# First-layer statistics and the block maxima of one matrix moved among the first products, and a wait ahead of the first weight split

## The chip, the cores and the metric

The kernel runs on one core of a Trainium2 chip. The metric is the device time of one execution in microseconds (us). The kernel before takes 1513.26 us, the median of 3 runs (1510.02 to 1513.64).

## The reference, cut to what matters

The program is a stack of four layers, each an attention and a feed-forward block with a layer norm ahead and a residual add behind, over x of 4 x 256 tokens x 512 features. The change touches two things: the first layer norm and attention (layer 0), and the dequantisation of the last feed-forward's weights (layer 3), which the kernel computes in the background of layer 0.

```python
def _layernorm(x, axis=-1, eps=1e-05):
    m = jnp.mean(x, axis=axis, keepdims=True)
    v = jnp.var(x, axis=axis, keepdims=True)
    return (x - m) / jnp.sqrt(v + eps)

def nf4_quant_dequant(w):                      # BLOCKSIZE = 64
    shape = w.shape
    flat = w.reshape(-1, BLOCKSIZE)
    absmax = jnp.max(jnp.abs(flat), axis=1, keepdims=True)
    normalized = flat / jnp.where(absmax == 0, 1.0, absmax)
    bounds = (NF4_CODE[:-1] + NF4_CODE[1:]) * 0.5
    idx = jnp.searchsorted(bounds, normalized)
    return (NF4_CODE[idx] * absmax).reshape(shape)

x = x + _L0_xattn_ref(_layernorm(x), ctx_4096, L0_xattn_Wq, L0_xattn_Wk, L0_xattn_Wv, L0_xattn_Wo)
...
dq1, dq2, dq3 = nf4_quant_dequant(w1), nf4_quant_dequant(w2), nf4_quant_dequant(w3)   # 1376 x 512 each
```

Layer 0's attention has 16 query heads in 4 groups of width 96, and each batch element has 256 + 64 keys.

## The kernel before

**Order of the work.** `schedule()` writes one list of steps by hand. Each engine walks that list and issues, in this order, what it has to do for a step. All engines are strictly in order on their own list and meet through semaphores. Tokens are in 8 tiles of 128, in two halves of 4 tiles. The list begins with `("stats", 0, 0)`, `("turn", 0, 0)`, six `v0` steps (value projections of four token tiles and two context parts), `k0`, `kc0` (keys of group 0), `q0` for 4 heads (numbered 0 to 3), and then the attention units n = 0, 1, 2, ...: `scores0` (scores on TensorE, maxima on VectorE, exp on ScalarE), `scale0` (VectorE), `turn0` (transposes on TensorE), `pv0`. After unit 2's scores the keys `k0` of the next group are computed. A `stats` step is VectorE work: `bn_stats` of 4 tiles, `bn_aggr`, a chain of about a dozen operations on 128 x 4 elements for 1/sqrt (the function `rsqrt`, lines 1199 to 1205), and the four normalisations into `xn` (line 1238). `turn` is transposes of `xn` on TensorE (line 1751), with a high part by ScalarE and a low part by VectorE (line 1194) into `xT`.

**Products.** Every fp32 product is done in three passes of rounded high and low parts (line 1724). So every weight chunk is loaded by SyncE into one of two staging buffers (line 743), its high part is made by ScalarE (line 951, `weight_high`), and its low part by GpSimd (line 858, `weight_low`). This pair is called a split. There are five slots for split chunks. SyncE issues the load of chunk i when chunk i-2 has its low part. Chunks 0 and 1 are the weights of `v0`, chunk 2 is the context, 3 and 4 are the weights of `k0`, `kc0` and `q0` of group 0, 5 and 6 those of group 1, 7 and 8 the output weights. `v0`'s first product waits for the low parts of both chunk 0 and chunk 1. The place of each split in the list is set by `spread_splits`: for the early ones, chunk i (i = 2 to 5) stands behind the list's entry number i-1, counted from zero, whatever that entry is.

**Background.** The dequantisation is a list `jobs`. For matrix m: `nf_row` (SyncE loads 128 rows, 256 KB, into one of four buffers; for the fifth row and on it waits until the maxima of four rows before are done, line 757), `nf_max` (VectorE, maxima of the 8 blocks of each row, line 1636; behind the last one a reciprocal, line 1641), `nf_turn` (TensorE transposes the maxima, line 2082, and waits for that reciprocal; ScalarE copies; SyncE stores them to HBM), `nf_scales` and `nf_load` (SyncE loads them back, broadcast, with the transposed weights, lines 792, 805, 807), then 15 `nf` steps for each of 33 tiles (VectorE, line 1664; ahead of the very first one 15 factor tiles `nf_d`, line 1647), each with an `nf_sum` product (TensorE, line 2093).

`with_background(base, "q0", BACKGROUND_END, jobs)` merges them into the list, starting behind the first `q0` step. Each step of the list has a room, each job a price (`NF_PRICE`: 1 for `nf`, 1.2 for `nf_max`, 6 for matrix 0's last one, 11 for the first `nf_load`, 0 for rows, `nf_turn` and `nf_scales`), and jobs are put in as long as what is paid is below the bill (the sum of prices) times the share of the room that is spent. The rooms sum to 511.64 and the bill to 550.4. That puts the eleven maxima of matrix 0 between the `q0` steps and ahead of the first scores, `nf_turn` for matrix 0 behind the next group's `k0`, and the first `nf` step behind the transposes of unit 3. `("stats", 0, 1)`, the statistics of x's second half, stands in the list ahead of `scores0` of unit 4.

Of the kernel before, what the change touches and what calls it, by code (L numbers as in the profile page):

```python
# [19 lines left out]
TPH = TILES // 2  # L20
BPH = B // 2
# [86 lines left out]
def schedule(only=None):  # L108

    steps = []  # L110


    steps += [("stats", 0, 0), ("turn", 0, 0)]
    steps += [("v0", 0, i) for i in range(TPH + BPH)]
    steps += [("k0", 0), ("kc0", 0)] + [("q0", 0, h) for h in range(HPG)]
    units = [(s, bl, h) for s in range(2 * G0) for h in range(HPG) for bl in range(BPH)]
    per, last_stage = HPG * BPH, 2 * G0 - 1
    for n in range(len(units) + PV_LAG):
        if n < len(units):
            steps.append(("scores0", n, *units[n]))  # L120
        if 1 <= n <= len(units):
            steps.append(("scale0", n - 1))
        if TURN_LAG <= n < len(units) + TURN_LAG:
            steps.append(("turn0", n - TURN_LAG, *units[n - TURN_LAG]))
        if n >= PV_LAG:
            steps.append(("pv0", n - PV_LAG, *units[n - PV_LAG]))
            if n - PV_LAG == G0 * per - 1:
                steps += [("v0", 1, i) for i in range(TPH + BPH)]
        if n < len(units):
            s, j = n // per, n % per  # L130
            if s < last_stage:
                late = 4 if s == G0 else 2
                if j == late:
                    steps.append(("k0", s + 1))
                if j == late + 1:
                    steps.append(("kc0", s + 1))
            if s >= 1 and j in (3, 4):
                steps += [("o0", s - 1, i) for i in (2 * j - 6, 2 * j - 5)]
            if s < last_stage and j >= 5:
                steps += [("q0", s + 1, h) for h in ((0, 1), (2,), (3,))[j - 5]]  # L140
            if (s, j) == (0, 3):
                steps.append(("stats", 0, 1))
            if (s, j) == (1, 2):
                steps.append(("turn", 0, 1))
            if (s, j) == (G0, 6):
                steps.append(("stats", 1, 0))
            if (s, j) == (G0 + 1, 6):
                steps.append(("turn", 1, 0))
# [204 lines left out]
def build(nc, a, out, known, only=None):  # L353
    ctx = ExitStack()
    with ctx:
        sig = Signals(nc, ctx, known)
# [36 lines left out]
        k0 = sb("k0", [HD0, 2, 2, BPH, KEYS0], F32R, s0)  # L393
# [186 lines left out]
        base = schedule(only)  # L580
        normalisations = [s[1:] for s in base if s[0] == "stats"]
        if only is None or only == 7:
            jobs = []
            jobs += [("nf_row", 0, f) for f in range(4)]
            for f in range(FT):
                jobs += [("nf_max", 0, f)] + [("nf_row", 0, f + 4)] * (f + 4 < FT)
            jobs.append(("nf_turn", 0))
            rest, rows = [], [("nf_row", m, f) for m in range(1, 3) for f in range(FT)]
            for m in range(1, 3):
                rest += [[("nf_max", m, f)] for f in range(FT)] + [[("nf_turn", m)]]  # L590
            rest[0] = rows[0:3] + rest[0]
            for entry in rest:
                if entry[-1][0] == "nf_max" and entry[-1][1:] != (1, 0):
                    i = (entry[-1][1] - 1) * FT + entry[-1][2]
                    entry[:0] = rows[i + 2:i + 3]
            items = [(m * FT + f, m, f) for m in range(3) for f in range(FT)]
            jobs += [("nf_scales", *items[0]), ("nf_load", *items[0])]
            sums = []
            for n, m, f in items:
                for j in range(1, NPART + 1):  # L600
                    jobs.append(("nf", n, m, f, j))
                    sums.append(("nf_sum", n, m, f, j))
                    if j > STAIR_RING - 1 or not n:
                        while len(sums) > STAIR_LAG:
                            jobs.append(sums.pop(0))
                    if j == 2 and n:
                        jobs += sums[:-2] + [("nf_end", *items[n - 1])]
                        sums = sums[-2:]
                    if j == 4 and n:
                        jobs.append(("nf_store", *items[n - 1]))  # L610
                    if j == 1 and n + 1 < len(items):
                        jobs.append(("nf_scales", *items[n + 1]))
                    if j == 6 and n + 1 < len(items):
                        jobs.append(("nf_load", *items[n + 1]))
                    if n >= REST_FROM and j % 5 == 4 and rest:
                        jobs += rest.pop(0)
            jobs += sums + [("nf_end", *items[-1]), ("nf_store", *items[-1])]
            base = with_background(base, "q0", BACKGROUND_END, jobs)
            assert base.index(("turn", 0, 1)) < base.index(("nf_row", 1, 0))
            assert base.index(("nf_turn", 2)) < base.index(("stats", 1, 0))  # L620
# [220 lines left out]
        def _(pool):  # L841
# [10 lines left out]
                    pool.dma_start(dst, src).then_inc(*sig.mark(f"loaded_{name}", 0, 16))  # L852

            def split(i):
                pool.wait_ge(*sig.when("weight_high", i))
                _, p, dims, *_ = chunks[i]
                hi, lo = weight(chunks[i][0], 0), weight(chunks[i][0], 1)
# [1321 lines left out]
```

## Time and profile before

| | |
|---|---|
| median of 3 runs | 1513.26 us |
| the profiled execution | 1513.1 us, span 1511.4 us |
| TensorE busy | 1366.7 us (90%) |
| VectorE busy | 1002.1 us (66%) |
| ScalarE, GpSimd busy | 474.3 us (31%), 328.1 us (22%) |
| mean granted TensorE clock | 0.949 |
| chain that ended last | PE 67%, DVE 18%, DMA 4% |

The span is the stretch from the first to the last instruction; the execution's own time is 1.7 us longer. In the rows PE is TensorE, DVE VectorE, ACT ScalarE, POOL GpSimd, SP SyncE. PEclk 1.00 is a granted clock of 2.4 GHz and 0.50 one of 1.2 GHz. The change lies wholly in the first 95 us of the list, so its own stage has to be read and not the averages.

### The profile page before, as it was taken

How to read it: one execution, taken by the hardware profiler on the slowest of the kernel's cores; microseconds unless marked ns; L12 is line 12 of the kernel's file. 1: busy time of each engine (PE TensorE's matmuls, PEld its weight loads, DVE VectorE, ACT ScalarE, POOL GpSimd, SP SyncE). 2: the span in 40 equal slices, each digit the busy share in tenths (PEclk: the TensorE clock that was granted, in tenths of full speed). 3: DMA queues.
4: the chain of work that ended last, by engine and by line, in shares of the span. 5: the costliest groups of instructions: out<-in, count | busy, mean ns of one | idle time of the engine just before them, and what ended most of it. 6: DMA issues, size and time to landing. Idle time of an engine off the chain costs nothing.

```text
span 1511.4 us, 18615 instructions
## 1 busy us (share of the span) xinstructions
PE 1366.7 (90%) x6429; PEld 1055.8 (70%) x6429; DVE 1002.1 (66%) x2200; ACT 474.3 (31%) x1004; POOL 328.1 (22%) x187
## 2 busy tenths in 40 slices
PE   6689999999999989997797889778999899999998
PEld 5467676777676766886675676556887677778886
DVE  3577878767878667876988667675446777444242
ACT  3333334333324233341344141322221443321010
POOL 4101211112111111342224140214443230012120
PEclk9889999999999999999899799879999999899999
DMA  4412433323322222332322220100112000011001
GB/s 153 144 39 77 112 116 111 107 77 95 90 80 78 68 77 83 86 113 86 109 81 82 85 84 1 56 29 16 43 54 70 28 29 2 1 49 63 25 20 56
DMA packets 112559, 104.86 MB, mean 69 GB/s; under 512 B 14674, under 2 KB 84194, under 8 KB 112466
## 3 DMA queue, kind: packets, MB, share of 16 engines
q1 hardware_dynamic: 111954, 102.81, 23.2%
q8 instruction: 54, 0.88, 0.2%
q0 software_dynamic: 512, 0.85, 0.2%
q14 instruction: 39, 0.32, 0.1%
HBM read 92.79 MB, written 10.82 MB: 69 GB/s over the span
## 4 chain that ended last, share of the span: by engine, by line
PE 67%; DVE 18%; DMA 4%; issue 3%; ACT 3%; SPq 3%; POOL 2%; ACTq 0%; DVEq 0%
PE bank L1724 49%; PE bank L2093 5%; PE bank L1818 4%; DVE nf_y L1664 4%; PE bank L2028 2%; PE bank L2048 2%; PE bank L1808 2%; POOL slots L858 2%; DVE xn L1238 1%; SPq L807 1%; PE bank L1751 1%; SPq L792 1%; ACT slots L951 1%; PE bank L2037 1%; DVE nf_w L1658 1%
## 5 line engine op out<-in xcount | busy, mean ns | idle before, releaser
L858 POOL TENSOR_TENSOR slots<-staging,slots 128x1024 fp32r<-128x1024 f32 (+5 forms) x114 | 269.0, 2364 | 1025.7 <-ACT slots L951 1025.7
L1724 PE MATMUL bank<-xT,slots 128*128 128x512 f32 (+1 forms) x1920 | 462.0, 398 | 4.5 <-DVE xT L1247 3.2
L1724 PEld LDWEIGHTS bank<-xT,slots 128*128 128x128 f32 (+1 forms) x1920 | 349.0, 183 | 103.5 <-issue 10.8
L1664 DVE TENSOR_SCALAR nf_y<-nf_w 128x512 fp32r<-128x512 f32 (+2 forms) x495 | 254.1, 550 | 21.1 <-PE bank L2093 20.0
L951 ACT ACTIVATE slots<-staging 128x1024 fp32r<-128x1024 f32 (+5 forms) x114 | 115.2, 1018 | 251.1 <-PE bank L1724 217.5
L2093 PE MATMUL bank<-nf_y,nf_d 128*128 128x512 f32 (+2 forms) x495 | 160.9, 418 | 36.2 <-DVE nf_y L1664 20.5
L1724 PE MATMUL bank<-slots,h 128*128 128x512 f32 (+1 forms) x728 | 178.9, 406 | 0.7 <-POOL slots L858 0.7
L1724 PEld LDWEIGHTS bank<-slots,h 128*128 128x128 f32 (+1 forms) x728 | 141.3, 195 | 36.3 <-issue 1.8
L2093 PEld LDWEIGHTS bank<-nf_y,nf_d 128*128 128x128 f32 (+1 forms) x495 | 92.1, 192 | 75.0 <-DVE nf_y L1664 39.1
L985 ACT ACTIVATE e<-bank,mx 128x320 f32<-128x320 f32 x128 | 66.4, 523 | 227.4 <-DVE mx L1275 225.3
L1294 DVE TENSOR_TENSOR x<-bank,x 128x512 f32<-128x512 f32 x56 | 38.7, 692 | 112.7 <-PE bank L1724 112.7
L1818 PE MATMUL bank<-eT,v 128*96 128x256 f32 (+1 forms) x384 | 109.3, 406 | 0.1
L1724 PE MATMUL bank<-slots,q 96*128 96x512 f32 x384 | 95.2, 397 | 0.0
L1194 DVE TENSOR_TENSOR q<-bank,q 96x256 fp32r<-96x256 f32 (+1 forms) x96 | 48.6, 506 | 57.8 <-ACT q L938 57.8
L1724 PEld LDWEIGHTS bank<-slots,q 96*128 96x128 f32 x384 | 71.8, 188 | 18.4 <-issue 1.5
L1818 PEld LDWEIGHTS bank<-eT,v 128*96 128x96 f32 (+1 forms) x384 | 57.0, 169 | 33.9 <-issue 24.7
L1751 PE MATMUL bank<-ident,xn 128*128 128x128 f32 x256 | 45.4, 323 | 34.7 <-DVE xn L1238 31.3
L1808 PE MATMUL bank<-ident,e 128*128 128x128 f32 x256 | 49.0, 287 | 28.0 <-DVE e L1282 25.8
L1724 PE MATMUL bank<-k,q 96*128 96x320 f32 x384 | 69.1, 316 | 3.3 <-DVE q L1194 3.1
L1724 PEld LDWEIGHTS bank<-k,q 96*128 96x128 f32 x384 | 61.8, 192 | 9.2 <-DVE q L1194 3.6
L1751 PEld LDWEIGHTS bank<-ident,xn 128*128 128x128 f32 x256 | 35.3, 163 | 45.3 <-issue 34.3
L938 ACT ACTIVATE q<-bank 96x256 fp32r<-96x256 f32 (+1 forms) x96 | 42.8, 449 | 62.4 <-PE bank L1724 58.6
(250 smaller groups left out, 1673.4 us busy)
## 6 DMA issues: line engine op xcount, KB each, us to landing
staging<-in_L_wqkT SPq DMA_DIRECT2D x16, 480.0 KB, 3.6
nf_out<-nf_w SPq DMA_DIRECT2D x30, 256.0 KB, 2.7
staging<-nf_out SPq DMA_DIRECT2D x30, 256.0 KB, 2.9
staging<-in_L_woT SPq DMA_DIRECT2D x16, 384.0 KB, 3.7
staging<-in_L_w SPq DMA_DIRECT2D x12, 512.0 KB, 3.7
nf_r<-nf_rcp SPq DMA_DIRECT2D x40, 128.0 KB, 3.1
nf_a<-nf_max SPq DMA_DIRECT2D x40, 128.0 KB, 3.5
xn<-in_L_w SPq DMA_DIRECT2D x20, 256.0 KB, 3.7
```

What stands on the lines that cost most here:

```text
L858: g.tensor_tensor(lo, split_source(i), hi.bitcast(FP32), ALU.subtract).then_inc(*sig.mark("weight_low", i))
L938: sc.activation(dst, src, func, **kw).then_inc(*sig.mark(f"{stage}_high", key))
L951: sc.activation(weight(name, 0), split_source(i), ACT.Copy).then_inc(*sig.mark("weight_high", i))
L985: sc.activation(e0[:, (2 * n + i) % E0_RING], psum(("scores0", n, i))[:, 0:KEYS0], ACT.Exp, bias=mx[:, n % 4, i:1 + i], accum_out=sm[:, n ...
L1194: v.tensor_tensor(dst, src, hi.bitcast(FP32), ALU.subtract).then_inc(*sig.mark(f"{stage}_low", key))
L1294: v.tensor_tensor(x[:, t], src, x[:, t], ALU.add).then_inc(*sig.mark(*mark))
L1664: v.tensor_scalar(nf_y[0:rows, i % STAIR_RING, 0:size], w_, bound, first, compare, ALU.mult)\
L1724: ins = mm(dst, l_, r_, start=begin and i == 0, stop=end and i == len(passes) - 1)
L1751: ins = nc.tensor.transpose(bank[:, i * P:(i + 1) * P], xn[:, i, c * P:(c + 1) * P], ident[:])
L1808: nc.tensor.transpose(b0[:, (2 * k + i) * P:(2 * k + i + 1) * P], e0[:, (2 * n + i) % E0_RING, k * P:(k + 1) * P], ident[:])
L1818: ins = mm(bank[0:HD0, 0:S], v0[0:p, t, g * HD0:(g + 1) * HD0], eT0[0:p, n % 2, k], start=k == 0, stop=k == 2)
L2093: mm(banks[NF_BANK][0:rows, 0:size], nf_d[0:rows, j - 1, 0:rows], nf_y[0:rows, i % STAIR_RING, 0:size], start=j == 1, stop=j == NPART).the ...
```

## The change

Three edits. `("stats", 0, 1)` moves from ahead of unit 4's scores to behind the third `v0` step. The 22 jobs `nf_row` and `nf_max` of matrix 0 are taken off the front of the background list and put by hand behind the first steps: four rows behind the first `v0` step; behind the fourth, fifth and sixth `v0` steps two maxima and two rows each; behind `k0` the maxima 6 and 7 with row 10 between them; behind `kc0` the maxima 8, 9 and 10. The rest of the list, beginning with `nf_turn`, is merged from the first `q0` step on as before, with a bill that is smaller by their prices. GpSimd's first split waits until the last tile of the first half is normalised.

```diff
-    steps += [("v0", 0, i) for i in range(TPH + BPH)]
+    steps += [("v0", 0, i) for i in range(3)] + [("stats", 0, 1)] + [("v0", 0, i) for i in range(3, TPH + BPH)]
...
-            if (s, j) == (0, 3):
-                steps.append(("stats", 0, 1))
...
             for f in range(FT):
                 jobs += [("nf_max", 0, f)] + [("nf_row", 0, f + 4)] * (f + 4 < FT)
+
+            places = {("v0", 0, 0): 4, ("v0", 0, 3): 4, ("v0", 0, 4): 4, ("v0", 0, 5): 4, ("k0", 0): 3, ("kc0", 0): 3}
+            base = [entry for s in base for entry in [s] + [jobs.pop(0) for _ in range(min(places.get(s, 0), len(jobs)))]]
+            assert not jobs
             jobs.append(("nf_turn", 0))
...
             def split(i):
+                if i == 0:
+                    pool.wait_ge(*sig.when("normalised", (0, TPH - 1)))
                 pool.wait_ge(*sig.when("weight_high", i))
```

## Rows read from the trace of the kernel before

**Rows 1.** Busy time by stretch: us, PE, PEld, DVE, ACT, POOL, PEclk, DMA share, GB/s.
```profile
45.80:60.20 14.40, 3.77 (x19) 2.89 (x18) 12.23 (x24) 3.42 (x9) 2.36 (x1) 0.63 0.62 199
60.20:63.30 3.10, 3.08 (x11) 2.45 (x12) 1.72 (x6) 2.36 (x9) 0.00 (x0) 0.51 0.00 0
...
73.80:79.30 5.50, 0.02 (x1) 0.05 (x1) 5.03 (x19) 1.24 (x5) 0.00 (x0) 0.78 0.34 94
79.30:87.10 7.80, 7.80 (x21) 4.84 (x22) 5.69 (x25) 3.15 (x10) 0.00 (x0) 0.50 0.06 19
```

**Rows 2.** Timeline, 45 to 80 us: start, length, engine, line, work, idle before it.
```profile
47.62 2.36 POOL L858 TENSOR_TENSOR slots<-staging,slots 96x1024 fp32r<-96x1024 f32 x1 [5.94 <-ACT slots L951]
...
48.58 0.67 DVE L1636 TENSOR_REDUCE nf_m<-nf_a 128x8 f32<-128x512 f32 x1
...
51.52 1.17 PE L1724 MATMUL bank<-k,q 96*128 96x320 f32 x3 [2.04 <-DVE q L1194]
...
57.24 0.70 DVE L1641 RECIPROCAL nf_m<-nf_m 128x88 f32<-128x88 f32 x1
57.86 1.61 DVE L1275 TENSOR_REDUCE mx<-bank 128x1 f32<-128x320 f32 x4
...
60.22 0.66 PE L1808 MATMUL bank<-ident,e 128*128 128x128 f32 x2 [7.52 <-DVE e L1282]
...
65.11 0.38 PE L2082 MATMUL bank<-ident,nf_m 128*88 128x128 f32 x2
...
70.21 2.46 DVE L1217 BATCH_NORM_STATS2 st<-x 128x6 f32<-128x512 f32 x4
...
72.62 1.23 SPq L807 DMA_DIRECT2D nf_a<-nf_max  x2
```

**Rows 3.** Timeline, 9 to 18 us, the end of the first statistics.
```profile
9.33 3.56 POOL L858 TENSOR_TENSOR slots<-staging,slots 128x768 fp32r<-128x768 f32 x2 [7.79 <-ACT slots L951]
9.34 1.82 DVE L1203 TENSOR_TENSOR rt<-rs 128x4 f32<-128x4 f32 x1
...
11.19 1.72 DVE L1204 TENSOR_TENSOR rt<-rt 128x4 f32<-128x4 f32 x1
...
13.15 1.91 DVE L1238 TENSOR_SCALAR xn<-x,mv,rs 128x512 f32<-128x512 f32 x4
...
17.80 9.06 PE L1724 MATMUL bank<-slots,xT 128*128 128x384 f32 x48
```

**Rows 4.** Timeline, 22 to 46 us, the first splits and products.
```profile
26.82 4.49 POOL L858 TENSOR_TENSOR slots<-staging,slots 128x960 fp32r<-128x960 f32 x2 [2.38 <-ACT slots L951]
...
30.86 2.95 PE L1724 MATMUL bank<-xT,slots 128*96 128x512 f32 x12
...
34.64 11.32 PE L1724 MATMUL bank<-xT,slots 128*96 128x512 f32 x48
```

**Rows 5.** DMA issues in 0 to 100 us: count, KB, median us to landing.
```profile
staging<-in_L_wqkT SPq DMA_DIRECT2D x6, 480.0 KB, 4.1
nf_w<-in_L_w SPq DMA_DIRECT2D x6, 256.0 KB, 3.8
...
x<-in_x SPq DMA_DIRECT2D x1, 1024.0 KB, 7.1
...
nf_a<-nf_max SPq DMA_DIRECT2D x4, 128.0 KB, 3.6
```

**Rows 6.** Timeline at 880 us: normalisations beside a split.
```profile
880.78 3.97 DVE L1238 TENSOR_SCALAR xn<-x,mv,rs 128x512 f32<-128x512 f32 x4
...
880.95 2.61 POOL L858 TENSOR_TENSOR slots<-staging,slots 128x1024 fp32r<-128x1024 f32 x1 [0.23 <-ACT slots L951]
```

**Rows 7.** Timeline, 82 to 91 us, the first background steps.
```profile
82.14 2.12 DVE L1647 TENSOR_SCALAR nf_d<-ident 128x128 fp32r<-128x128 f32 x15
...
84.18 0.69 DVE L1658 TENSOR_TENSOR nf_w<-nf_w,nf_r 128x512 f32<-128x512 f32 x1
...
89.48 1.08 DVE L1664 TENSOR_SCALAR nf_y<-nf_w 128x512 fp32r<-128x512 f32 x3
```

**Rows 8.** Waits of TensorE, 110 to 620 us: total, times, longest.
```profile
PE bank L1808 <- DVE e L1282: 12.8, 12, 1.9
```

## The prediction

> **What bounds the kernel now.** I first looked at the busy time by engine: TensorE is busy for 90% of the span and most of the chain that ended last, so what counts is the time that TensorE loses, by idling or by running at the lower granted clock. Then I cut the first 95 us into stretches [rows 1]. From 45.8 to 60.2 us TensorE is busy for 3.8 of 14.4 us, and VectorE for 12.2. The timeline shows why [rows 2]: the eleven block maxima, fed by row loads, stand on VectorE ahead of the maxima of the first scores, and the reciprocal behind them ends at 57.9 us. Only then come four score maxima, and TensorE's first transposes start at 60.2. From 73.8 to 79.3 TensorE idles again: the statistics of the second half, begun at 70.2 us, stand ahead of a score maximum [rows 1, 2]. Behind each hole the granted clock is at its lower level, 1.2 GHz (0.50): until 63.3 us, and from 79.3 to 87.1 [rows 1]. A third loss is at the start: the first product begins at 17.8 us, and just before, two VectorE operations on 128 x 4 elements took 1.82 and 1.72 us beside GpSimd's two splits [rows 3], where their like takes 0.16 to 0.17.
>
> I count in lost TensorE time, against the profiled execution of 1513.1 us. It lies 0.2 us below the median of the runs, so no correction is needed.
>
> **What the change takes away.**
> - Start. Without the splits beside them the two slow operations take 0.17 each, so the normalisations end 3.2 us earlier, at 15.06 - 3.2 = 11.9. The two splits, 3.56 us together [rows 3], now begin there and end at 15.5. The first product needs both, and starts at 15.6 in place of 17.8 (its other input, the transposed x, is ready from about 13.8): 2.2 us gained.
> - The hole from 45.8 to 60.2: 14.4 - 3.8 = 10.6 us idle, and 0.6 us, half of the 1.17 that three products of unit 2 took there at the lower clock [rows 1, 2].
> - The lower clock behind it, half of 3.1: 1.5. The hole of the statistics: 5.5. The lower clock behind that one, half of 7.8: 3.9 [rows 1].
>
> Together 2.2 + 10.6 + 0.6 + 1.5 + 5.5 + 3.9 = 24.3 us.
>
> **What it adds: the transposes of the maxima.** Pricing the maxima at nothing has a consequence that decides the sum. They are no longer in the background list, so that list begins with `nf_turn`, of price 0, and it is placed directly behind the first `q0` step. TensorE is in order: `q0` for heads 1 to 3 and all scores are queued behind a wait for the reciprocal of the eleven maxima. So I must find when that is ready.
>
> - Loads on SyncE. The low part of chunk 1 is done at 15.5, then chunk 3 and the 1 MB rest of x are issued; the latter lands 7.1 us later [rows 5], at 23.0. The context's split ends at about 21, chunk 3's at 23.2, chunk 4's (issued at 21, 3.6 us to land, 1 us on ScalarE, 2.25 us on GpSimd, half of 4.49 [rows 4]) at 27.9, and chunk 5's at 30.2. Row 0 is issued behind the load of chunk 5, at 23.7, row 1 behind that of chunk 6 at 28.3, rows 2 and 3 behind that of chunk 7, which waits for chunk 5's low part, at 30.6 and 31.1. At 3.8 us each [rows 5] rows 2 and 3 land at 34.5 and 35.
> - Statistics on VectorE. They begin at 23.0, `bn_stats` takes 2.46 [rows 2] and the aggregation 0.4, to 25.9. Then the small operations meet the splits of chunks 4, 5 and 6 (25.65 to 27.9, 28 to 30.2, 32.6 to 34.85). If each split holds VectorE as in [rows 3], the small ones end at 32.4. The normalisations are held too: four took 3.97 us beside a split at 880 us [rows 6] in place of 1.91 [rows 3]. They end at 36.0. If nothing held them all would end at 30.1.
> - Maxima. They are not held: one took 0.67 us inside a split at 47.6 [rows 2]. From 36.0 the first four end at 38.7. Row 6 is issued when maxima 2 are done, 38.1; it lands at 42, maxima 6 end at 43.3; row 10 follows chunk 9's load at 43.8, lands at 47.6, its maxima end at 48.3 and the reciprocal at 49.2. With statistics that end at 30.1 the landing of row 2 at 34.5 sets it, and the reciprocal ends at 45.8; with each of the three landings in this chain 1 us slower, at 52.
>
> The first `q0` step ends at about 35.3: before, `k0`, `kc0` and it took from 30.86 to 37.5 [rows 4], now they start at 28.6 (`v0` needs 13.1 us as before, and chunk 4 is ready at 27.9). So TensorE idles for 49.2 - 35.3 = 13.9 us, with 10.5 and 16.7 as ends. The load that the maxima hide behind is hidden, but TensorE is stopped for them in another place.
>
> The GPSIMD Engine Reference of the Trainium skill (section 8, Key points) says that GpSimd shares its SBUF interfaces with VectorE, with contention for instructions in a 2-port mode or with two SBUF inputs. It speaks against this change, since it would hold the moved statistics; the trace agrees for two-input operations (1.82 us) and for normalisations (3.97 us for four). By that rule the reciprocal comes at 49.2, without it at 45.8.
>
> **What it adds: the first background steps.** The bill falls by 10 x 1.2 + 6 = 18, to 532.4, or 1.041 per unit of room. The three remaining `q0` steps have 3.12 of room each, so at the fourth, 12.48 x 1.041 = 13.0 exceeds `nf_load`'s 11 and two `nf` steps stand ahead of the first score maxima; before, they stood behind unit 3. VectorE meets their weights there. From `nf_turn` (65.1) to the landing of the last broadcast (issued up to 73.85, and 3.6 to land) were about 11.7 us [rows 2, 5], so they are there at 61. TensorE ends the three `q0` steps (2.83 each [rows 4]) at 49.2 + 0.4 + 8.5 + 2.7 for the lower clock = 60.8. Copy and low part of the last follow to 62.1, and then 2.12 us for the factor tiles, to 64.2 [rows 7]: the landing is hidden. To the first transposes: 0.69 for the scaling, five `nf` steps of 0.36 that stand before and between the maxima [rows 7], and 2.36 us from the first score maximum to the transposes as before (57.86 to 60.22 [rows 2]), 4.9 in all, to 69.1. TensorE has scores and two sums until 64.0: idle for 5.1 us. The clock: a restart cost 1.5 us once and 3.9 the other time [rows 1]; I take 2.7 behind each of the two holes.
>
> Added: 13.9 + 2.7 + 5.1 + 2.7 = 24.4. The sum is 24.4 - 24.3 = +0.1, and the time 1513.2 us. The `nf` steps and sums that now run between 65 and 95 us are no cost: they are missing later. Over the rest of the background each step of the list carries 3.3% fewer of them. TensorE waits 12.8 us there for `scale0`, which `nf` steps delay [rows 8]; a thirtieth of that is 0.4. Which `nf` step meets which split changes throughout; the longest such wait was 1.9 us, and I allow 2.5 either way.
>
> **Rivals.**
> - Faster, 0.27: the statistics mostly miss the splits and the clock returns as after 60.2. Then 10.5 + 1.5 + 5.1 + 1.5 = 18.6 against 24.3, 5.7 less, 1507.4. For it: `nf_max` and `bn_stats` are insensitive, and the places depend on when x lands. Against it: three splits lie within 9 us, just where the small operations are.
> - Slower, 0.27: `nf_turn` is the new barrier and comes late. SyncE queues rows among four chunk loads, which wait for splits, and landings of 4.1 and 7.1 us show that big loads slow each other [rows 5]. With the reciprocal at 52 and 3.9 us for each restart: 16.7 + 3.9 + 5.1 + 3.9 = 29.6, 5.3 more, 1518.4. Every us by which the reciprocal comes later costs one; at the clock costs of my sum it is slower by over 0.3% from 53.6 us on, at the larger ones from 51.2.
> - The wait doesn't do what it says, 0.06: if the small operations were slow for another reason, the splits would start at 15.1 and the first product at 18.7, 3.1 us later than in my sum: 1516.3.
>
> **How the numbers follow.** My forecast, 0.40: 1513.2, with 1509 to 1517 as its own range. The range over the cases runs from 1504.9 (the faster case less 2.5) to 1519.8 (the slower one and 1.4). What this measurement can tell from no change is about 0.3%, 4.5 us. Faster: the 0.27, and 0.06 from the edge of the forecast, 0.33. Slower: 0.22 of the slower case, and 0.04 from the others, 0.26. The rest, 0.41, is no change.
>
> **What would show it.** In the trace after: the first product near 15.6 us; the statistics of the second half end between 30 and 36, with long small operations; TensorE idle from about 35 until line 2082 near 49; a second hole of about 5 us ahead of the first transposes near 69, with the factor tiles between; no hole for statistics behind unit 2. I am wrong if `nf_turn` isn't what stops TensorE, if the reciprocal is ready before 44 or after 54, or if the time differs while the first 100 us do not.

## The result, and the profile after

The kernel after takes 1502.88 us, the median of 9 runs (1499.56 to 1508.47), against 1511.31 us (1507.69 to 1514.86) for the kernel before on the same chip: a ratio of 0.9946 [0.9929, 0.9962]. That is 0.54% faster, 8 us, where I forecast no change and a range that ended at 1504.9. The profiled execution after took 1502.41 us, so the traces differ by 10.7 us; in what follows they are compared with each other, and every such difference carries the scatter of two single executions. How large that can be is shown under the last experiment: two executions with the same list up to a point reached it 9.2 us apart. From the page after (busy us, share of the span, instructions; then shares of the chain that ended last):

```profile
span 1500.7 us, 18616 instructions
PE 1359.8 (91%) x6429; PEld 1049.6 (70%) x6429; DVE 1004.3 (67%) x2200; ACT 473.5 (32%) x1004; POOL 331.5 (22%) x187
PE 65%; DVE 20%; ACT 4%; DMA 4%; issue 3%; SPq 2%; POOL 2%; ACTq 0%; DVEq 0%
```

In the code after, line numbers from 858 on are 4 higher than before (L1724 is L1728, L1664 is L1668, L2082 is L2086), and those of SyncE's loads 2 higher (L807 is L809). The start, from the timeline after (start, us, engine, line, operation, what ended the idle time before it); it answers to [rows 2, 3]:

```profile
9.84 0.16 DVE L1207 TENSOR_TENSOR rt<-rs 128x4 f32<-128x4 f32 x1
12.43 3.59 POOL L862 TENSOR_TENSOR slots<-staging,slots 128x768 fp32r<-128x768 f32 x2 [10.89 <-DVE xn L1242]
16.12 8.58 PE L1728 MATMUL bank<-slots,xT 128*128 128x384 f32 x48 [0.86 <-POOL slots L862]
26.86 2.24 POOL L862 TENSOR_TENSOR slots<-staging,slots 128x960 fp32r<-128x960 f32 x1 [2.96 <-ACT slots L955]
26.92 2.20 DVE L1207 TENSOR_TENSOR rt<-rs 128x4 f32<-128x4 f32 x1
30.53 2.17 DVE L1209 SCALAR_TENSOR_TENSOR rs<-rt,rs 128x4 f32<-128x4 f32 x1
32.74 1.92 DVE L1242 TENSOR_SCALAR xn<-x,mv,rs 128x512 f32<-128x512 f32 x4
48.23 0.70 DVE L1645 RECIPROCAL nf_m<-nf_m 128x88 f32<-128x88 f32 x1
48.98 0.66 PE L2086 MATMUL bank<-ident,nf_m 128*88 128x128 f32 x2 [12.93 <-DVE nf_m L1645]
61.01 4.53 POOL L862 TENSOR_TENSOR slots<-staging,slots 96x1024 fp32r<-96x1024 f32 x1 [21.00 <-ACT slots L955]
63.37 2.79 DVE L1668 TENSOR_SCALAR nf_y<-nf_w 128x512 fp32r<-128x512 f32 x2
69.39 0.66 PE L1812 MATMUL bank<-ident,e 128*128 128x128 f32 x2 [2.94 <-DVE e L1286]
```

The barrier of the forecast is there: TensorE idles 12.93 us ahead of line 2086 (13.9 forecast), and the moved statistics meet the splits (2.20 and 2.17 us for operations that take 0.16 alone). The stretches around both new holes (us, then busy us and instructions of PE, PEld, DVE, ACT, POOL, granted clock, share of the DMA engines, GB/s), which answer to [rows 1]:

```profile
35.50:49.00 13.50, 0.57 (x4) 0.12 (x2) 8.40 (x15) 1.70 (x3) 4.09 (x2) 0.62 0.72 231
49.00:53.40 4.40, 4.40 (x14) 3.08 (x15) 0.47 (x1) 0.44 (x2) 0.00 (x0) 0.60 0.09 20
62.00:69.40 7.40, 0.59 (x2) 0.23 (x2) 7.33 (x19) 2.25 (x8) 3.53 (x1) 0.78 0.34 101
69.40:73.00 3.60, 3.60 (x12) 2.78 (x13) 2.03 (x7) 2.62 (x7) 0.00 (x0) 0.50 0.01 1
73.00:100.00 27.00, 27.00 (x143) 20.10 (x142) 18.18 (x51) 11.19 (x33) 2.26 (x1) 1.00 0.27 74
```

The second hole is 6.8 us of 7.4, and the granted clock is back at 1.00 from 73.0. So the start went nearly as forecast, and the gain isn't there. I read the same event in both traces (for a unit, its first score maximum) and took the difference; minus is earlier than the kernel before:

```
event (time before, us)    after  e4_old  e5_merge  e1_old  e2_old  e3_no  e7_price  e9_price  e6_turn
                                  _merge  _alone    _stats  _maxima _wait  12        20        _late
unit 8 (110.7)             +3.1   -4.9    +18.0     +12.8   -9.8    +4.0   +5.9      +1.3      -12.4
unit 32 (314.1)            -4.9   -4.3    +9.9      +4.7    -8.3    -4.1   -4.1      +5.2      -14.9
first up0 step (617.4)     -1.7   -2.7    +13.4     +5.2    -5.4    -0.9   -4.1      +7.1      -15.7
867.0                      -10.2  -3.9    +5.2      -3.0    -7.9    -9.4   -13.5     +1.7      -23.6
end (1511.4)               -10.7  -4.2    +4.4      -3.7    -9.3    -10.0  -14.3     +1.3      -27.6
```

At unit 8 the kernel after is 3.1 us behind, and at 867, some 10 us behind the last of the background's sums, 10.2 ahead. All of the gain, 13.3 us, lies in between, where I had priced the change at 0.4. The same stretch in both kernels (columns as above), before and then after:

```profile
110.70:867.00 756.30, 694.97 (x3230) 527.20 (x3229) 578.80 (x1247) 268.82 (x628) 151.01 (x70) 0.96 0.32 91
```

```profile
113.90:856.80 742.90, 687.94 (x3215) 521.76 (x3214) 570.85 (x1229) 267.97 (x628) 152.11 (x70) 0.97 0.32 91
```

TensorE idles for 61.3 us before and 55.0 after, 6.4 less, and is busy for 7.0 less. It has 17 sums fewer to do here (476 before, 459 after, by line 2093 and its like), done ahead of unit 8; I price them at 4.1 (17 at 0.24, line 1728's busy time over its number on the page, an estimate). The remaining 3 go with the clock, 0.97 for 0.96.

### The profile page after: what moved, and what is told of

Same layout as the page of the kernel before. It is cut to its first block, busy times and chain, and to the rows that moved or that the text cites. A ratio compares the mean times of both kernels' runs of the same rounds, so it can differ in the third digit from the quotient of the medians.

```text
span 1500.7 us, 18616 instructions
## 1 busy us (share of the span) xinstructions
PE 1359.8 (91%) x6429; PEld 1049.6 (70%) x6429; DVE 1004.3 (67%) x2200; ACT 473.5 (32%) x1004; POOL 331.5 (22%) x187
## 4 chain that ended last, share of the span: by engine, by line
PE 65%; DVE 20%; ACT 4%; DMA 4%; issue 3%; SPq 2%; POOL 2%; ACTq 0%; DVEq 0%
PE bank L1728 47%; PE bank L2097 6%; DVE nf_y L1668 5%; PE bank L1822 4%; PE bank L2032 2%; POOL slots L862 2%; PE bank L2052 2%; PE bank L1812 1%; DVE xn L1242 1%; SPq L809 1%; ACT slots L955 1%; PE bank L2041 1%; DVE st L1315 1%; DVE x L1300 1%; DMA nf_a<-in_L_w 1%
## 5 line engine op out<-in xcount | busy, mean ns | idle before, releaser
L1728 PE MATMUL bank<-xT,slots 128*128 128x512 f32 (+1 forms) x1920 | 462.3, 398 | 6.1 <-DVE xT L1251 3.3
L1728 PEld LDWEIGHTS bank<-xT,slots 128*128 128x128 f32 (+1 forms) x1920 | 349.1, 183 | 103.8 <-issue 11.5
L1668 DVE TENSOR_SCALAR nf_y<-nf_w 128x512 fp32r<-128x512 f32 (+2 forms) x495 | 257.6, 553 | 16.6 <-PE bank L2097 15.4
L1728 PE MATMUL bank<-slots,h 128*128 128x512 f32 (+1 forms) x728 | 179.6, 407 | 0.0
L1728 PEld LDWEIGHTS bank<-slots,h 128*128 128x128 f32 (+1 forms) x728 | 142.0, 196 | 35.2 <-issue 0.4
L1822 PE MATMUL bank<-eT,v 128*96 128x256 f32 (+1 forms) x384 | 105.5, 395 | 1.1 <-ACT eT L999 1.1
L1728 PE MATMUL bank<-slots,q 96*128 96x512 f32 x384 | 95.0, 396 | 0.6 <-DVE q L1198 0.6
L1728 PEld LDWEIGHTS bank<-slots,q 96*128 96x128 f32 x384 | 71.8, 188 | 18.5 <-issue 1.7
L1728 PE MATMUL bank<-k,q 96*128 96x320 f32 x384 | 66.8, 310 | 0.0
L1728 PEld LDWEIGHTS bank<-k,q 96*128 96x128 f32 x384 | 61.0, 188 | 4.7 <-issue 0.7
L1621 DVE TENSOR_TENSOR g<-bank,g 128x512 f32<-128x512 f32 (+1 forms) x22 | 15.2, 691 | 67.2 <-PE bank L1728 67.2
```

What stands on the lines that cost most here:

```text
L1668: v.tensor_scalar(nf_y[0:rows, i % STAIR_RING, 0:size], w_, bound, first, compare, ALU.mult)\
L1728: ins = mm(dst, l_, r_, start=begin and i == 0, stop=end and i == len(passes) - 1)
L1822: ins = mm(bank[0:HD0, 0:S], v0[0:p, t, g * HD0:(g + 1) * HD0], eT0[0:p, n % 2, k], start=k == 0, stop=k == 2)
```

## The experiments

**Placement undone, placement alone.** Which part moves the middle: the edited start, or the new places of the background steps that follow from it?

```
after, NF_PRICE:   ("nf_load", 0, 0): 11   ->  29        (e4_old_merge: nf steps where they stood before)
before, NF_PRICE:  ("nf_max", 0, 10): 6    ->  **{("nf_max", 0, f): 0 for f in range(11)}
                                                         (e5_merge_alone: nf steps where they stand after)
```

> The changed kernel with the price of the first nf_load raised from 11 to 29, which is the 18 that the moved maxima took out of the bill. From the first nf step on, the background is then merged with the foreground exactly as in the kernel before (same bill, same places), while the early statistics, the early maxima, nf_turn behind the first q0 and the wait of the first split stay. Theory START (the gain comes from the lost TensorE time of the first 100 us, as my accounting had it): the hole of 13.9 us and one restart stay, the second hole of about 5 us ahead of the first transposes goes, so the trace is 24.3 - 16.6 = 7.7 us ahead of the kernel before at unit 8 and keeps that to the end: 1503.6. Theory MERGE (in the changed kernel the start brings about nothing and its lead arises later, between 100 and 870 us, because the background is merged otherwise, thinner and begun 20 us earlier): here no lead arises between unit 8 and 870 us, in particular none of the 8.6 us that the changed kernel wins from 617 to 867 us; whatever lead there is at unit 8 is the lead at the end.

> The kernel before with price 0 for the eleven maxima of matrix 0. They then stand, with nf_turn, behind the first q0 step, and from the first nf step on the background is merged exactly as in the changed kernel; statistics, maxima and first split are where the kernel before has them. It starts late: TensorE stands at nf_turn from 37.5 to about 58, the first transposes come near 78 in place of 60, and the hole of the second statistics stays. START: the trace is 14 to 18 us behind the kernel before at unit 4 and stays so, 1525 to 1529. MERGE: as far behind at unit 4, but from there it gains as the changed kernel does from unit 4 to 870 us (from +3.7 to -10.2 there, 14 us), and ends near 1512; the part from 617 to 867 us alone gives 8 us.

Measured: 1507.55 us, 0.9966 [0.9948, 0.9985], and 1517.12 us, 1.0027 [1.0011, 1.0043]. From unit 8 to 867, by the table, the old places give +1.0 behind the new start, the new places -12.8 behind the old start, and both together -13.3. In e4_old_merge all 495 `nf` steps stand among the other steps where they stood before; in e5_merge_alone 482 stand where they stand after, and 13 one step off. So the middle goes with the places of the background steps and hardly with anything that the change does at the start, and the merge theory is borne out in both. What a kernel has won or lost at unit 8 it keeps when the places are the same: e4_old_merge is 4.9 us ahead of the kernel before there and 4.2 at the end (7.7 were expected), the kernel after is 14.8 ahead of e5_merge_alone there and 15.1 at the end. In e5_merge_alone the start is worse by 18 us, since the maxima, with `nf_turn` behind them, then stand at one place behind the first `q0` step, where nothing has prepared them: TensorE waits 19.35 us for their reciprocal.

**The parts of the start.**

```
e1_old_stats:   steps += [("v0", 0, i) for i in range(TPH + BPH)]   and the stats step back ahead of unit 4's scores
e2_old_maxima:  the two lines `places` and `base` left out
e3_no_wait:     -   if i == 0:
                -       pool.wait_ge(*sig.when("normalised", (0, TPH - 1)))
```

> The changed kernel with the second half's statistics back ahead of unit 4's scores; the rest as changed. START: the maxima no longer stand behind the statistics, so the reciprocal comes some 2.4 us earlier, but the hole of 5.5 us and the restart of 3.9 us behind the statistics return: +7.0 us on the changed kernel, 1510. MERGE: the background is merged as in the changed kernel and the later gain stays; the hole costs the same 5.5 to 9.4 us early on. If the later stages have slack that absorbs it (TensorE waits for VectorE anyway), it ends within 3 us of the changed kernel.

> The changed kernel without the hand-made places: rows and maxima of matrix 0 are merged behind the q0 steps as in the kernel before, with the bill of before; early statistics and the wait stay. START: first product 2.2 us earlier, no hole and no restart for the statistics (9.4 us): 11.6 us off 1511.3, so 1499.7, which is faster than the changed kernel by 3 us. MERGE: only what the start gives, which it expects to be partly given back, and nothing from 617 to 867 us: 1503 to 1508.

> The changed kernel without GpSimd's wait ahead of the first split. START: the two small operations of the first statistics take 1.8 and 1.7 us again and the first product starts at 17.8 in place of 16.1; the loads of chunks 2 and 3 and the rest of x are issued 2.5 us earlier, though, so the statistics of the second half start earlier, and the reciprocal that sets nf_turn comes 0 to 2 us earlier. TensorE stands there anyway, so the wait is worth nothing: the time is that of the changed kernel within 2 us, and the trace has nf_turn at 47 to 49. If the wait is worth its 2.2 us, 1505.

Measured: 1507.48, 0.9968 [0.9952, 0.9985]; 1503.07, 0.9929 [0.9901, 0.9957]; 1502.71, 0.9945 [0.9926, 0.9963]. The moved statistics are worth 9.7 us up to unit 8 (+12.8 without them, +3.1 with them); at the end e1_old_stats is 7.0 us behind the kernel after in the traces, as the start theory expected, and 3.3 by the ratios, nearer to the merge theory.

With the maxima put back, unit 8 comes 12.9 us earlier (-9.8), but that run puts the `nf` steps back as well. Against e4_old_merge, where only the maxima and `nf_turn` are moved (-4.9), 4.9 us of the 12.9 are the barrier's, and the other 8.0, of which 4.1 are sums done early, belong to the earlier `nf` steps. All 495 `nf` steps of e2_old_maxima stand where they stood in the kernel before, and its lead of 9.8 us is still 9.3 at the end: here a gain of the start reached the time, as the start theory said.

The wait is worth 0.9 at unit 8 and nothing in the time; the first product gains with it, but the reciprocal, which ends the first hole, comes 0.8 us later without it and not earlier. Nor does it come earlier without the moved statistics. It begins at 48.23 in the kernel after; here first in e3_no_wait, then in e1_old_stats:

```profile
49.04 0.70 DVE L1643 RECIPROCAL nf_m<-nf_m 128x88 f32<-128x88 f32 x1
```

```profile
49.23 0.70 DVE L1647 RECIPROCAL nf_m<-nf_m 128x88 f32<-128x88 f32 x1
```

**Fewer steps ahead of the splits?** If the middle gains because every list step carries 3.3% fewer background steps, the gain must follow the bill: at price 12 it is 533.4 of the old 550.4 (3.1% fewer), at 20 it is 541.4 (1.6% fewer, half the effect).

```
after, NF_PRICE:   ("nf_load", 0, 0): 11   ->  12  (e7_price12)   and   20  (e9_price20)
```

> The changed kernel with the price of the first nf_load 12 in place of 11. The first nf steps of each tile keep their foreground places or move by one, and nine splits move by one or two steps of the list. THIN (the gain between unit 8 and 867 us comes from a background that is begun earlier and is 3.3% thinner): nearly the changed kernel again, the trace's lead over the kernel before within 1.5 us of -10.2 at 867 us. LUCK (the gain hangs on which background step happens to stand beside which wait): it moves by 3 us or more somewhere on the way, and the end lies anywhere between -13 and 0.

> The changed kernel with that price 20: half way from the changed merge (11) to the old one (29), and the first nf step stands behind the next group's k0, after the first score maxima. Start: as with 29, the hole ahead of the first transposes is some 3 us shorter than in the changed kernel, -3 to -5 us at unit 8 with half of the nf steps done ahead (2 us of TensorE). THIN: from unit 8 to 867 us it gains half of what the changed kernel gains there (13.3 of which 3.9 are the sums done ahead), so 6 to 7, and ends at -9 to -11, about as the changed kernel. LUCK: that gain isn't between the two ends but may be 0 or 12.

Measured: 1499.33, 0.9927 [0.9908, 0.9945], and 1510.35, 0.9995 [0.9979, 1.0010]. From unit 8 to 867 price 12 gives -19.4 and price 20 gives +0.4, where half of 13.3 was due. That theory fell: the effect doesn't follow the bill. With price 20 unit 8 also came 1.3 us late, where 3 to 5 early were expected, and between 110 and 180 us TensorE stands once for 5.3 us behind an `nf` step's copy, where the longest such wait of the kernel before is 1.4 (engine, line, waited for: us, times, longest):

```profile
PE bank L2097 <- DVE nf_y L1668: 5.3, 1, 5.3
```

**Where in the middle.** The table has 8.5 of the 13.3 us between the first `up0` step and 867. Two kernels change over there from one placement to the other, by a function that joins two merged lists (the steps that one has and the other hasn't yet are put in at the joint):

```
def with_two_merges(steps, cut, prices, firsts, last, jobs):
    ...
    head, tail = a[:a.index(cut)], b[b.index(cut):]
    gone, due = set(head), [s for s in b[:b.index(cut)] if s[0].startswith("nf")]
    ...
before: base = with_two_merges(base, ("up0", 4, 0), ({}, {("nf_max", 0, f): 0 for f in range(11)}), ...)   (e10_tail_new)
after:  base = with_two_merges(base, ("up0", 4, 0), ({}, {("nf_load", 0, 0): 29}), ...)                   (e11_tail_old)
```

> The kernel before, with its list unchanged up to the fifth up0 step of the first half (at about 640 us); there four nf steps and their sums are put in at once, and behind it the background stands as in the changed kernel. Nothing of the change's first 100 us is in it. MERGE in this stage: the changed kernel's gain between 617 and 867 us (8.5 us by the traces; 8.2 and 8.2 in the two experiments with its merge) comes from these four steps and what they shift, so this kernel's trace is level with the kernel before until 640 us and 7 to 9 us ahead at 867 us: 1503. If the gain there needs the history (what is late when the stage begins), it is 0 to 3 us.

> The changed kernel with its list unchanged up to the same up0 step, and the background as in the kernel before behind it. MERGE: level with the changed kernel until 640 us, there some 2 us ahead of the kernel before, and no further gain up to 867 us: 0 to -4 us at the end, 1509. If the changed kernel's gain belongs to its start, it keeps -10.

Measured: 1508.08, 0.9959 [0.9941, 0.9978], and 1508.03, 0.9955 [0.9935, 0.9974]. From the first `up0` step to 867 the new tail behind the old head goes from +2.4 to -5.4, and the old tail behind the new head from -3.9 to -5.1. The placement behind `up0` alone is thus worth some 7 to 8 us, with four `nf` steps of difference, as the merge theory expected. (The lists ahead of the joint are those of the kernels before and after; that e10_tail_new is 2.4 us late at the first `up0` step and e11_tail_old 2.2 us earlier than the kernel after is scatter.) A stretch with the same content in all four kernels, from the 9th to the 13th `up0` step, in the order before, after, e10_tail_new, e11_tail_old:

```profile
666.20:742.70 76.50, 62.08 (x258) 48.48 (x257) 56.29 (x97) 19.33 (x30) 21.09 (x9) 0.91 0.31 92
```

```profile
664.80:735.30 70.50, 62.05 (x255) 48.25 (x253) 52.56 (x95) 19.37 (x30) 20.60 (x9) 0.93 0.37 107
```

```profile
670.10:741.00 70.90, 60.84 (x255) 47.40 (x254) 52.69 (x95) 19.47 (x29) 20.18 (x9) 0.94 0.36 107
```

```profile
661.30:737.60 76.30, 63.41 (x259) 49.43 (x257) 56.31 (x97) 19.29 (x29) 21.27 (x9) 0.89 0.32 92
```

The stretch takes 76.5 and 76.3 us with the old placement, 70.5 and 70.9 with the new. In the kernels before and after TensorE is busy for as long, and idle for 14.4 and 8.5. In the pair with joined lists only 2.8 us of the 5.4 are idle time (12.9 against 10.1); the rest goes with a clock of 0.89 against 0.94. For the first pair the waits and the timeline name the place. Before (the wait; SyncE's load of tile 28 with its ten broadcasts; then VectorE's first operation on each of two tiles, and what it waited for):

```profile
PE bank L1751 <- DVE xn L1238: 6.4, 1, 6.4
...
692.79 0.34 SPq L805 DMA_DIRECT2D nf_w<-in_L_w3T  x1
693.17 5.82 SPq L807 DMA_DIRECT2D nf_a<-nf_max  x10
...
700.48 0.69 DVE L1658 TENSOR_TENSOR nf_w<-nf_w,nf_r 128x512 f32<-128x512 f32 x1 [3.61 <-DMA nf_a<-nf_max]
...
717.77 0.69 DVE L1658 TENSOR_TENSOR nf_w<-nf_w,nf_r 128x512 f32<-128x512 f32 x1 [5.25 <-DMA nf_a<-nf_max]
```

And after:

```profile
PE bank L1755 <- DVE xn L1242: 0.5, 1, 0.5
...
685.22 0.50 SPq L807 DMA_DIRECT2D nf_w<-in_L_w3T  x1
685.77 5.83 SPq L809 DMA_DIRECT2D nf_a<-nf_max  x10
...
693.09 0.69 DVE L1662 TENSOR_TENSOR nf_w<-nf_w,nf_r 128x512 f32<-128x512 f32 x1 [4.12 <-DMA nf_a<-nf_max]
...
709.96 0.69 DVE L1662 TENSOR_TENSOR nf_w<-nf_w,nf_r 128x512 f32<-128x512 f32 x1 [4.82 <-DMA nf_a<-nf_max]
```

The list packs the `nf` steps here, so one tile follows another at the pace of SyncE's ten issues (5.8 us), their landing and VectorE. Counted from the start of the stretch, tile 28's load is issued at 26.6 us before and at 20.4 after, since in the list after this load stands ahead of the first `down0` step and in the list before behind it. VectorE waits for its broadcasts in either, but 6 us earlier after, and what is queued behind on VectorE, the adds, statistics and normalisations of the next layer norm, comes 6 us earlier with it: TensorE waits 0.5 us for `xn` and not 6.4. This wait differs between single traces too: it is 4.7 in e4_old_merge and 4.6 in e11_tail_old (old placement), 0.6 in e5_merge_alone and 3.4 in e10_tail_new (new placement). It is shorter with the new one, by 1.2 to 5.9 us.

**How much does any shift do?** A control was missing: the kernel before with the same knob moved by one.

```
before, NF_PRICE:  ("nf_load", 0, 0): 11   ->  12  (e8_before12)
```

> The kernel before with the price of the first nf_load 12 in place of 11; all nf steps keep their places or move by one, some splits move by one or two steps. LUCK: the old merge is an arrangement as sensitive as the new one, and this moves it by 2 to 7 us, either way (1504 to 1518). If the old merge is slow for a reason of its own (29 units of price ahead of the first step, a thicker background), it stays within 2 us, 1511.

Measured: 1500.24, 0.9907 [0.9882, 0.9932], the largest surprise here. Among the other steps of the list six splits move by one to three entries, 129 of the 495 `nf` steps come one to three entries later and 366 stay, and the kernel before is 0.93% (14 us) faster, more than the whole change brings. Its stretch from unit 8 to 867:

```profile
111.70:856.20 744.50, 687.64 (x3232) 519.76 (x3231) 578.95 (x1247) 268.31 (x628) 150.74 (x70) 0.98 0.32 92
```

The instructions are the same within two of 3230, TensorE idles 56.9 us, 4.5 less, and its busy time falls by 7.3, with the granted clock at 0.98 for 0.96. So I moved the price in both kernels:

```
before and after, NF_PRICE:  ("nf_load", 0, 0): 11   ->  10 and 13   (before10, before13, after10, after13)
```

> The kernel before with the price of the first nf_load 10. LUCK: the kernel before at 11 is one arrangement among others (12 gave -14 us), so 10 and 13 fall between, at -15 to +3 us from 1511; and averaged over 10 to 13 the changed kernel is no more than 2 us faster than the kernel before. GAIN: 12 was the exception, 10 and 13 lie within 3 us of the kernel before.

> The kernel before with that price 13. As for 10: LUCK -15 to +3 us from 1511, GAIN within 3 us of it.

> The changed kernel with that price 10. LUCK: it scatters by some 5 us about the same mean as the kernel before's arrangements; as 11 and 12 gave 1502 and 1499, worse ones than these must come, 1503 to 1512. GAIN: it lies with its fellows, 1498 to 1504.

> The changed kernel with that price 13. As for 10: LUCK 1503 to 1512, GAIN 1498 to 1504.

```
price           10                        11                      12                       13                       mean
before          1.0003 [0.9982, 1.0024]   1                       0.9907 [0.9882, 0.9932]  0.9950 [0.9929, 0.9971]  0.9965
after           0.9874 [0.9847, 0.9900]   0.9946 [0.9929, 0.9962] 0.9927 [0.9908, 0.9945]  1.0003 [0.9984, 1.0023]  0.9938
barrier late    0.9904 [0.9874, 0.9934]   0.9883 [0.9856, 0.9910] -                        0.9889 [0.9855, 0.9923]  0.9892
```

Over four neighbouring prices the two kernels differ by 0.28%, 4 us, with a scatter of 0.46% among the ones and 0.53% among the others (standard deviations), which makes 0.35% on the difference. At price 13 the kernel after is the slower one by 0.5%. The measured 0.54% is one draw of this. Both theories had bounds too narrow: at price 10 the kernel after fell below either (1492 on the scale of 1511), before13 is 8 us below 1511, where GAIN allowed 3, and the mean differs by 4 us, where LUCK allowed 2.

**The barrier moved.** The last row of that table is the kernel after with the background beginning behind the first scores in place of the first `q0` step, so that `nf_turn` stands behind work that TensorE can do meanwhile.

```
-            base = with_background(base, "q0", BACKGROUND_END, jobs)
+            base = with_background(base, "scores0", BACKGROUND_END, jobs)
```

> The changed kernel with the background merged from the first scores0 step on in place of the first q0, so nf_turn stands behind the scores of unit 0 and not behind the first q0. START: TensorE does the other q0 steps and the first scores while the maxima run; it stops only from about 44.5 to the reciprocal at 48.9, the score maxima follow at once and the first transposes come at about 51.5, where the changed kernel has 69.4 and the kernel before 60.2. With no hole for the statistics the trace is 16 to 18 us ahead of the kernel before at unit 4, and the later merge (1.067 per unit of room) lies between the two: about -15 at the end, 1496. If the first 100 us don't count, because later waits swallow a lead, it ends near the changed kernel, 1503.

> The kernel with nf_turn behind the first scores, with the price of the first nf_load 10. The start is 9 to 13 us ahead of the kernel before at unit 8 whatever the price, and the merge adds between 0 and -15: 1487 to 1502. If its lead were luck, one of the two prices would bring it above 1502.

> The kernel with nf_turn behind the first scores, with the price of the first nf_load 13; the same bounds as with 10, 1487 to 1502 us, and above 1502 if its lead were the luck of one arrangement.

Measured: 1494.42 (1485.51 to 1498.4), 0.9883; 1495.56, 0.9904; 1494.9, 0.9889, intervals in the table. The trace of e6_turn_late is of its fastest execution, 9 us below the median, so its column in the table of events shows more than this kernel gains on the median. From its timeline:

```profile
50.09 0.70 DVE L1645 RECIPROCAL nf_m<-nf_m 128x88 f32<-128x88 f32 x1
51.39 1.97 PE L1728 MATMUL bank<-k,q 96*128 96x320 f32 x6 [5.38 <-DVE q L1198]
53.15 0.63 PE L2086 MATMUL bank<-ident,nf_m 128*88 128x128 f32 x2
56.41 0.41 PE L1812 MATMUL bank<-ident,e 128*128 128x128 f32 x2 [0.30 <-DVE e L1286]
```

The reciprocal is as late as ever, 50.79, and TensorE doesn't stand for it. The hole that is left, 5.38 us, is `q`'s low part, queued on VectorE behind the maxima. The first transposes are at 56.41 (51.5 expected) against 69.39, and at unit 8 the kernel is 15.5 us ahead of the kernel after. Its three prices lie within 0.21% of each other, and their mean is 0.73% (11 us) below the mean of the kernels before; price by price it is 0.99, 1.17 and 0.61% below them. So the change with this barrier moved gains over the kernel before at all three prices tried. Price 12, the kernel before's best (0.9907), wasn't tried with it. What the barrier's place alone is worth is less sure: against the kernel after it is 0.30% slower at price 10, and 0.63 and 1.14% faster at 11 and 13, on the mean 0.49% with a scatter of 0.73%, which makes 0.42% on that mean. That isn't clear of the luck of the placement.

I also put the tail of price 12 behind that start, from `up0` on:

```
after: base = with_two_merges(base, ("up0", 4, 0), ({}, {("nf_load", 0, 0): 12}), ("scores0", "q0"), ...)
```

> The kernel with nf_turn behind the first scores (29 us ahead in one trace, ratio 0.988) up to the same up0 step, and behind it the background of the kernel with price 12, which won 9.4 us from 617 to 867 us. The kernel with the late nf_turn was 15.7 us ahead at 617 us and won 7.9 from there to 867. If the stages add: 25 us ahead at 867 us, 1.5 us better than it, 1492 to 1494. If the last stage is decided by what it meets, anywhere from 15 to 28 us ahead.

Measured: 1495.37, 0.9863 [0.9833, 0.9894], the same as e6_turn_late within the intervals, which can't tell the 1.5 us that the sum of the stages would add. In its trace the last stage does what it did in the kernel with price 12: from the first `up0` step to 867 it wins 9.0 us, and 9.3 there. What differs is the part ahead of the joint, by the events as above:

```
event (time before, us)    e6_turn_late  e12_late_turn_tail  late10  late13
unit 8 (110.7)             -12.4         -9.2                -12.5   -12.2
unit 32 (314.1)            -14.9         -5.9                -7.1    -14.6
first up0 step (617.4)     -15.7         -6.5                -16.2   -8.0
867.0                      -23.6         -15.5               -20.4   -12.9
end (1511.4)               -27.6         -15.8               -20.4   -16.7
```

Up to the joint the list of e12_late_turn_tail is that of e6_turn_late, loads and splits included, and in both traces every engine has the same instructions in the same order. They are 3.2 us apart at unit 8, 9.0 at unit 32 and 9.2 at the first `up0` step all the same. So this is the scatter between two executions, and both kernels have it in their times (1485.51 to 1498.4 and 1485.1 to 1497.59). Single traces often agree far better: from unit 8 to 867 the three with the places of the kernel after (after, e5_merge_alone, e3_no_wait) differ from the kernel before by -13.4, -12.8 and -13.4 us. But a difference of a few us between two traces needs the medians, or a second trace, beside it.

## Why the prediction was wrong

Its steps at the start held, in part because misses cancelled. The first product comes at 16.12 (15.6), the reciprocal at 48.93 (49.2), the first hole is 12.93 us (13.9), the first transposes are at 69.39 (69.1). Smaller terms missed both ways: the normalisations ran between two splits and ended at 34.7 (36.0), which the landing of the later rows made worth nothing; the second hole was 6.8 (5.1), because two factor-scaled copies took 2.79 us beside a split; and two restarts of the clock cost about 1.8 each and not 2.7 (4.4 and 3.6 us at 0.60 and 0.50). At unit 8 the trace is 3.1 us behind, of which 4.1 are sums done early: -1.0, where the sum said +0.1. One reading was off without effect: from `nf_turn` at 65.1 to the landing of the last broadcast (73.85 and 3.6) are about 12.3 us and not 11.7, which the copies on VectorE hide as well. The faster rival's price, 5.7 us at the start, didn't come about either.

The rule of the GPSIMD Engine Reference (the Trainium skill, section 8, Key points) stands by the rows: two-input operations of 128 x 4 elements took 2.20 and 2.17 us beside splits of 2.24 and 2.26. It decided less than I gave it, as the late rows and not the statistics set the reciprocal: with the statistics moved back (e1_old_stats) it begins at 49.23, no earlier than 48.23.

The wait did what it says and was worth nothing, which the sum had as a gain of 2.2: e3_no_wait is 0.9 us later at unit 8. The first product's 1.7 us are swallowed by the hole that the reciprocal ends.

What failed is the last step, the price of the changed merge over the rest of the background: "a thirtieth of that is 0.4", and "I allow 2.5 either way". It measured -13.3 us from unit 8 to 867, or -9.2 without the returned sums. Nor does the change lie wholly in the first 95 us of the list, as I wrote ahead of the prediction: 451 of the 495 `nf` steps stand up to twenty entries earlier among the other steps, most of them far behind unit 8. I had taken the longest wait of one kind, 1.9 us [rows 8], as the bound for this reshuffle of the background among the splits. Other waits in the same stretch are far longer, and each depends on which step stands ahead of which. The one that I priced went the other way, from 12.8 to 17.7 us. Between unit 8 and 867, before and then after:

```profile
PE bank L2093 <- DVE nf_y L1664: 20.5, 10, 6.5
PE bank L2093 <- DVE nf_w L1674: 15.4, 4, 7.1
PE bank L1808 <- DVE e L1282: 12.8, 12, 1.9
```

```profile
PE bank L2097 <- DVE nf_y L1668: 22.2, 8, 8.4
PE bank L1812 <- DVE e L1286: 17.7, 17, 2.4
PE bank L2097 <- DVE nf_w L1678: 6.4, 5, 3.2
```

The whole range of ±2.5 was too narrow by more than a factor of four: the same stretch, with hardly anything moved at the start, moved by -11.8 on a change of one price by one. A smaller part of the miss is the base: I counted from 1513.1, and the median of nine runs of the kernel before is 1511.31, so 1.8 of the 10.3 us between 1513.2 and 1502.88 lie there.

What stays open: what the change as it stands gains apart from the luck of its placement. Four arrangements of each don't tell 4 us from none. With the `nf` steps held in their old places its start gains 0.34% (e4_old_merge, 0.9966 [0.9948, 0.9985]), and the statistics and the wait without the moved maxima gain 0.71% (e2_old_maxima, 0.9929), but the change as written moves them. Of the 8.5 us behind the first `up0` step 6 are traced to a wait in this pair of traces; in other pairs that wait differs by less. The other 2.5, the 4.8 spread over the attention units ahead of it, and the 14 us of e8_before12, I can only describe by idle time and clock, not assign step by step.

## What to carry to other kernels

A change that adds to or takes from a list which a planner merges moves everything behind it; before a gain is credited to the edit, move the planner's knob by one in both kernels and compare the rows. To price the edit alone, hold the merged steps in their old places: then the lead at unit 8 was, within about 1 us, the lead at the end. Read two traces at events of the same content, find the stretch that holds the difference before explaining it, and don't build on a few us of one trace. A step of price 0 is not free if an in-order engine must wait for its input: `nf_turn` stopped TensorE for 12.93 us, and with it a few entries later the changed kernel was faster than the kernel before at each of three prices, though against the kernel after only at two of them.

## What the runs showed that I had not expected

- A price of 12 for 11 in the kernel before, with the same instructions, took 0.93% (14 us) from the time; ratios of neighbouring prices spread over 1.3% in the kernel after (0.9874 to 1.0003).
- The clock amplifies such shifts. Between unit 8 and 867 the granted clock was 0.96 before and 0.98 in e8_before12, and TensorE's busy time for the same products (3230 and 3232 instructions) went from 694.97 to 687.64 us, while idle time fell by 4.5.
- A split delays even the smallest two-input operation to its own end: 128 x 4 elements begun at 26.92 ended at 29.12, the split at 29.10.
- One list gives executions that differ by many us at the same event: 9.2 us at the first `up0` step between e6_turn_late and e12_late_turn_tail. From 867 us to the end four traces take 640.4 to 640.9 us (e6_turn_late, late13, before10, e8_before12) and all others 642.8 to 644.4; no run shows why. So some 3 of the 14 us of e8_before12's trace lie there, and 11.8 in its merged middle.
